# A four-layer kernel on one core: attention 0's keys are made ahead and its loop is unrolled; attention 1 sends its queries three units ahead instead of two

## The chip, the core and the metric

The kernel runs as one program on one core of a Trainium2 chip. Its engines run beside each other and meet only at semaphores: TensorE (PE, with its weight loads as PEld), VectorE (DVE), ScalarE (ACT), GpSimd (POOL) and SyncE (SP), which here only issues transfers. The metric is the time of one execution in microseconds (us). A difference of about 0.2% is what a measurement of this kernel can tell from none.

## The reference, cut to what matters

The input x is 4 batches of 512 tokens by 512 columns, the context 4 by 512 by 128. Four residual layers follow each other:

```python
x = x + tanh(g_xattn[0]) * attention_0(layernorm(x), ctx)
x = x + tanh(g_ffn[0])   * mixture_0(layernorm(x))      # 8 experts, 2 per token
x = x + tanh(g_xattn[1]) * attention_1(layernorm(x), ctx, ctx)   # 16 heads of 32
x = x + tanh(g_ffn[1])   * mixture_1(layernorm(x))      # 16 experts, 6 per token

def attention_0(p, k_v):            # per batch
    kv  = k_v @ W_k.T + b_k                             # 512 x 128
    sim = (p @ kv) @ kv.T * 512**-0.5                   # 512 x 512
    return softmax(layernorm_over_columns(sim) * gamma + beta)

def attention_1(q, k, v):           # 4 groups of 4 heads share keys and values
    probs = softmax(q_h @ k_g.T / sqrt(32))
    return concat(probs @ v_g) @ Wc.T + bc
```

## The kernel before, in words

**Order of work.** Each layer is a block with one program for each engine, written out by hand; an engine works through its own list and waits for semaphores by count. A block begins when all engines have left the one before. PSUM is one tile `ps` of eight banks.

**Attention 0** goes batch by batch (b = 0 to 3). VectorE first makes the layer norm's statistics of all four batches (`row_stats`: four BATCH_NORM_STATS, some operations on 128x4, and a square root that ScalarE makes in `deviation`). For a batch, `keys` makes kv: PE multiplies (L415), ScalarE adds the bias (L348), takes the mean (L351) and centres the keys (kc, L357), PE turns kv (L418) and ScalarE copies it (L353). ScalarE normalises the rows of x (xn, L130), PE turns them (L425) and ScalarE copies them to pT (L363). The product with kv (L429) is copied to oT (L367), and PE multiplies it with kc to scores in banks 0 to 3 (L436). ScalarE squares them (L373) and takes the deviation (L376); VectorE scales and shifts (L455, L461) and makes the negative maxima (nmx, L465); ScalarE takes the exponential (L381); VectorE adds the result to x (L476). PE's body is a hardware loop over b with keys, turn, product and scores in this order. In ScalarE's loop body the keys and pT of batch b+1 come between deviation and exponential of batch b. The keys and turned rows share banks 4 to 7. GpSimd meanwhile splits the first seven of the experts' weight chunks into high and low parts (L168 to L182) and SyncE stores them. Nothing in this attention prepares the layer norm of mixture 0: that block's own start makes the statistics of its batches (`NORMED` is 0 for mixture 0 and 3 for mixture 1).

**Mixture 0** begins with columns(0) (rows normalised by ScalarE, turned by PE, split into xhi and xlo), the router's logits(0) (L1526), the copy of these (lgT, L1347), columns(1) (L1537) and then the shared expert's products (L1558 up, L1576 down). After these come blocks of gathered tokens (L1634, L1650, L1669) with weights fetched expert by expert.

**Attention 1** has 16 units: unit u is batch u // 4 and group u % 4. A unit takes eight steps j. In a step ScalarE takes two exponentials (L792, L796), GpSimd subtracts for the low half (L738), and PE makes the next scores (L843), two raw products for maxima (L828, read by VectorE's reductions L972), and products with the values (L857). Three parts run ahead of their unit:

- the queries: GpSimd normalises the group's columns (xc, L686 and L694, step 5), PE turns them (L817, step 0), ScalarE makes qhi (L756, step 1), VectorE qlo (L961, step 2), and SyncE copies both into `qs` by three transfers (`strips`, L622 and L625). Unit u does this for u+2, and GpSimd's part for u+3.
- the raw products of unit u+2 begin at step 4 of unit u, and wait there for these transfers;
- the maxima of unit u+1 are turned at step 4 (L833), split, and sent by two transfers (L632) that the first scores of unit u+1 wait for.

Buffers of xc, qhi and qlo are two deep by group parity. `qs` has room for all 16 heads, so a unit's strips lie in the place of the unit four before it. During units 0 to 3 and 12 to 15 a second stream splits and stores the last 16 weight chunks.

Of the kernel before, what the change touches and what calls it, by code (L numbers as in the profile page):

```python
# [15 lines left out]
P = 128  # L16
B, S, D = 4, 512, 512
NT = B * S // P
TB = S // P
# [201 lines left out]
def cross_attention_0(nc, a, sb, g):  # L221
# [3 lines left out]
    with ExitStack() as ctx:  # L225
# [13 lines left out]
        kv = sb(ctx, "a0_kv", [P, TB, DC])  # L239
# [3 lines left out]
        kc = sb(ctx, "a0_kc", [P, S])  # L243
# [12 lines left out]
        def sem(name):  # L256
# [3 lines left out]
        gates_ready, gamma_done, nmean_ready, kc_ready = (  # L260
            sem(n) for n in ("gates", "gamma_done", "nmean", "kc"))
# [10 lines left out]
        with nc.Block() as block:  # L272
# [64 lines left out]

            def normalise_scalar(act, b):
                act.wait_ge(g["s_ln"], b + 1)
                for t in range(TB):  # L340

                    act.wait_ge(xn_read, TB * b + t + 1)
                    g["normalise"](act, xn, t, TB * b + t, 0, xn_ready)

            def keys_scalar(act, b):

                act.wait_ge(kvT_mm, b + 1)
                act.activation(kvT[:], ps[:, 4, :], ACT.Identity, bias=bk[:, 0:1],  # L348
                               accum_out=ksum[:]).then_inc(kvT_ready, 1)
                act.wait_ge(kvT_ready, b + 1)  # L350
                act.mul(nmean[:], ksum[:], -1.0 / S).then_inc(nmean_ready, 1)  # L351
                act.wait_ge(kv_tr, b + 1)
                act.copy(kv[:].rearrange("p t d -> p (t d)"), ps[:, 5, :]).then_inc(kv_ready, 1)  # L353

                act.wait_ge(nmean_ready, b + 1)
                act.wait_ge(sim_ready, TB * b + TB)
                act.activation(kc[:], kvT[:], ACT.Identity, bias=nmean[:, 0:1]).then_inc(kc_ready, 1)  # L357

            def turn_scalar(act, b):

                act.wait_ge(xn_read, TB * b + 2 * TB)
                for k in range(KD):
                    act.copy(pT[:, k, :], ps[:, 4 + k, :]).then_inc(pT_ready, 1)  # L363
# [5 lines left out]
            def deviation_scalar(act, b):  # L369
                for t in range(TB):  # L370

                    act.wait_ge(sim_ready, TB * b + TB + t + 1)
# [12 lines left out]
            def _(act):  # L385
                act.wait_ge(eps_set, 1)
                g["deviation"](act, 0, 0)
                act.wait_ge(par_in, PARAMS)
                normalise_scalar(act, 0)
# [8 lines left out]
                with act.Fori(0, B - 1) as b:  # L398
                    normalise_scalar(act, b + 1)
                    deviation_scalar(act, b)  # L400
                    keys_scalar(act, b + 1)
# [1786 lines left out]
```

## Time and profile before

| | |
|---|---|
| median of 3 runs | 2252.59 us (2250.19 to 2254.02) |
| profiled execution, its own time | 2243.46 us |
| its span | 2241.7 us |
| PE busy | 1911.8 us (85%) |
| POOL, DVE, ACT busy | 1004.7, 1167.9, 861.3 us |
| mean granted clock of TensorE | 0.925 of full speed |

The profiled execution is one run, and the others are timed without a profile. Busy shares are averages over four layers with different limits; the stages are: attention 0 to 123.4 us, mixture 0 to about 682, attention 1 to about 1172, mixture 1 to the end. An idle time in a row is the time the engine stood still before that instruction, with what ended it. "x4" marks merged instructions: the time is then that of the group.

### The profile page before, as it was taken

Reading aid. Unit: us, or ns where it says so; the run is one execution under the profiler, and the core shown is the slowest. Engines: PE = TensorE matmul, PEld = TensorE weight load, DVE = VectorE, ACT = ScalarE, POOL = GpSimd, SP = SyncE. Lnnn points to the kernel's source line nnn. Section 1 sums busy time; section 2 is a strip of 40 time slices with the busy share of each in tenths; the row PEclk is TensorE's granted clock in tenths of the full one; section 3 lists DMA queues with packets and bytes.
Section 4 is the critical chain, followed back from the end, with each engine's and each line's share of the span. In section 5 each row is a group of like instructions: output and inputs, shape, how many; then the busy total and the mean of one; then the engine's idle time right before and its main releaser. Section 6 shows DMA issues by size and latency. Waiting matters only on the chain. (4 is left out here: it accounts for less than half of the span.)

```text
span 2241.7 us, 36800 instructions
## 1 busy us (share of the span) xinstructions
PE 1911.8 (85%) x10825; PEld 1567.9 (70%) x10825; DVE 1167.9 (52%) x2331; ACT 861.3 (38%) x1403; POOL 1004.7 (45%) x735
## 2 busy tenths in 40 slices
PE   3758999979892777888868899999999979999995
PEld 2347787757671455555546777799999879899994
DVE  5474654423334896878973766444444334344442
ACT  3752221123341676767655123133333223233331
POOL 4344655625454787889631001143433323333331
PEclk9779999988895798998989999999999989999998
DMA  9367666988887574323642000766469895754444
GB/s 337 122 218 242 184 205 226 294 295 240 257 197 169 151 227 98 47 42 51 190 150 83 29 31 1 264 178 158 88 176 334 265 304 128 187 130 83 78 79 111
DMA packets 131457, 372.67 MB, mean 166 GB/s; under 512 B 20456, under 2 KB 24424, under 8 KB 126104
## 3 DMA queue, kind: packets, MB, share of 16 engines
q1 hardware_dynamic: 80504, 260.69, 36.3%
q0 software_dynamic: 33600, 79.73, 18.6%
q10 hardware_dynamic: 17184, 30.09, 3.8%
q8 instruction: 96, 1.57, 0.3%
q14 instruction: 73, 0.60, 0.1%
HBM read 209.93 MB, written 151.86 MB: 161 GB/s over the span
## 5 line engine op out<-in xcount | busy, mean ns | idle before, releaser
L1650 PE MATMUL ps<-f_wb,f_xThi 128*128 x2088 | 537.7, 339 | 29.9 <-issue 26.8
L1774 POOL DMA_INDIRECT y_scratch<-f_yo,f_rows x150 | 238.7, 1591 | 479.0 <-issue 264.1
L1650 PEld LDWEIGHTS ps<-f_wb,f_xThi 128*128 128x128 f32 x2088 | 372.0, 193 | 41.3 <-issue 32.3
L1650 PE MATMUL ps<-f_wb,f_xTlo 128*128 x1044 | 346.7, 332 | 0.0
L738 POOL TENSOR_TENSOR a_elo<-a_e,a_ehi 128x1024 f16<-128x1024 f32 x128 | 282.8, 2222 | 87.0 <-ACT a_ehi L796 85.0
L1669 PE MATMUL ps<-f_wb,f_hThi 128*128 (+2 forms) x822 | 276.9, 418 | 7.3 <-DVE f_hTlo L2049 7.3
L2067 DVE TENSOR_TENSOR f_g<-ps,f_bb 128x352 f32<-128x352 f32 x111 | 58.3, 525 | 337.2 <-PE ps L1650 334.4
L1747 POOL DMA_INDIRECT f_xg<-xn_scratch,f_rows x150 | 160.0, 1067 | 158.7 <-PE ps L1634 119.3
L1650 PEld LDWEIGHTS ps<-f_wb,f_xTlo 128*128 128x128 f32 x1044 | 200.9, 192 | 0.0
L1485 ACT ACTIVATE f_yo<-ps,f_share 128x512 f32<-128x512 f32 x150 | 103.2, 688 | 249.2 <-PE ps L1669 191.3
L972 DVE TENSOR_REDUCE a_nmax<-ps 128x1 f32<-128x512 f32 x256 | 163.9, 680 | 56.4 <-PE ps L828 56.0
L1558 PE MATMUL ps<-f_xhi,f_w13hi 128*128 128x512 f32 x448 | 175.7, 392 | 0.0
L1558 PE MATMUL ps<-f_xlo,f_w13hi 128*128 128x512 f32 x448 | 174.8, 390 | 0.0
L1558 PE MATMUL ps<-f_xhi,f_w13lo 128*128 128x512 f32 x448 | 174.7, 390 | 0.0
L1669 PEld LDWEIGHTS ps<-f_wb,f_hThi 128*128 128x128 f32 (+2 forms) x822 | 142.4, 191 | 42.3 <-issue 24.0
L1576 PE MATMUL ps<-f_w2hi,f_act_parts 128*128 128x512 f32 x448 | 153.0, 409 | 21.2 <-DVE x_res L2015 20.5
L828 PE MATMUL ps<-a_ks,a_qs 96*128 96x512 f32 x256 | 114.4, 515 | 61.1 <-DMA a_qs<-a_qlo 41.9
L792 ACT ACTIVATE a_e<-ps 128x1024 f32<-128x1024 f32 x128 | 132.7, 1036 | 82.5 <-PE ps L843 81.0
L1473 ACT CAST f_xThi<-ps 128x512 fp32r<-128x512 f32 x150 | 88.1, 587 | 195.1 <-PE ps L1634 187.7
L1669 PE MATMUL ps<-f_wb,f_hTlo 128*128 (+2 forms) x411 | 162.2, 395 | 0.0
L1479 ACT CAST f_hThi<-ps 128x384 fp32r<-128x384 f32 (+1 forms) x150 | 67.4, 449 | 207.5 <-PE ps L1659 202.7
L2049 DVE TENSOR_TENSOR f_hTlo<-ps,f_hThi 128x384 fp32r<-128x384 f32 (+1 forms) x150 | 78.4, 523 | 113.7 <-ACT f_hThi L1479 111.6
(242 smaller groups left out, 3654.1 us busy)
## 6 DMA issues: line engine op xcount, KB each, us to landing
f_wb<-w_scratch SPq DMA_DIRECT2D x16, 2816.0 KB
w_scratch<-f_stage_up SPq DMA_DIRECT2D x27, 1024.0 KB
w_scratch<-a_stage_up SPq DMA_DIRECT2D x23, 1024.0 KB, 5.3
f_stage_raw<-in_f_w_dram SPq DMA_DIRECT2D x29, 768.0 KB, 7.2
f_wb<-w_scratch SPq DMA_DIRECT2D x16, 1024.0 KB
w_scratch<-f_stage_down SPq DMA_DIRECT2D x108, 128.0 KB
f_wb<-w_scratch SPq DMA_DIRECT2D x8, 1536.0 KB
a_later_raw<-in_f_w_dram SPq DMA_DIRECT2D x16, 768.0 KB, 5.2
```

The source lines that it names most:

```text
L738: pool.tensor_tensor(l, e, h, ALU.subtract).then_inc(lo_pool, 1)
L792: act.activation(e32[:, j % 4, :, :], ps[:, 2 * (j % 2):2 * (j % 2) + 2, :], ACT.Exp)
L828: pe.matmul(ps[:, A_BANK + n % 2, :], qs[0:3 * HD, HPG * grp + q, P * t:P * t + P], ks[0:3 * HD, grp, :], start=True, stop=True).then_inc( ...
L972: dve.tensor_reduce(nmax[:, grp % 2, n:n + 1], ps[:, A_BANK + n % 2, :], AX.X, ALU.max, negate=True).then_inc(max_done, 1)
L1473: act.copy(xThi[:, b % 2, :, :].rearrange("p k t -> p (k t)"), ps[:, XB, :]).then_inc(xT_hi, 1)
L1485: act.activation(yo[:, b % 3, :], ps[:, OB + b % 2, :], ACT.Identity, scale=share[:, b:b + 1]).then_inc(yo_ready, 1)
L1558: mm = pe.matmul(ps[:, 2 * h + w, :], wt[:, h, w, k, :], xt[:, k, S * t:S * t + S], start=(m == 0), stop=(m == 3 * KD - 1))
L1576: mm = pe.matmul(ps[:, bank(c), :], at[:, t % 2, h, P * c:P * c + P], wt[:, h, :], start=(m == 0), stop=(m == 5))
L1650: mm = pe.matmul(out, xt[:, b % 2, k, :], weights(at, w, k, low), start=(m == 0), stop=(m == 3 * KD - 1))
L1669: mm = pe.matmul(ps[:, OB + b % 2, :], ht[0:n, b % 2, P * j:P * j + P], wb[0:n, bass.ds(at + 512 * NB + 1024 * j + 512 * low, D)], start=( ...
L1747: pool.indirect_dma_start(xg[:, b % 3, :], None, xn_d, bass.IndirectOffsetOnAxis(ap=rows_of[:, b:b + 1], axis=0), bounds_check=ROWS + SPAR ...
L1774: pool.indirect_dma_start(y_d, bass.IndirectOffsetOnAxis(ap=rows_of[:, b:b + 1], axis=0), yo[:, b % 3, :], None, bounds_check=ROWS + SPARE ...
```

## The change

1. **Attention 0's keys.** kv and kc get one place for each batch. PE makes keys 0 and 1, turns batch 0, and makes keys 2 and 3, all ahead of the first product; the keys use banks 4 to 7 in pairs, and batch 0 is turned into banks 0 to 3.
2. **Attention 0's loops** are written out (no hardware loop) on PE, ScalarE and VectorE. Batch b+1 is turned right behind the scores of batch b. A product waits for one k of pT at a time. VectorE's second pass waits tile by tile.
3. **Statistics for mixture 0.** VectorE makes `row_stats(1, b-1)` at the head of batch b, ScalarE its root beside the deviation of batch b. `NORMED` is 3 for both mixtures, so mixture 0's block makes only those of batch 3.
4. **Attention 1's queries** run one unit further ahead: unit u turns, splits and sends u+3, and GpSimd normalises u+4. Ahead of unit 0 three units are prepared instead of two.

```diff
-        kv = sb(ctx, "a0_kv", [P, TB, DC])
+        kv = sb(ctx, "a0_kv", [P, B, TB, DC])
-        kc = sb(ctx, "a0_kc", [P, S])
+        kc = sb(ctx, "a0_kc", [P, B, S])
...
             def deviation_scalar(act, b):
...
+                if b > 0:
+                    g["deviation"](act, 1, b - 1)
                 act.wait_ge(squared, TB * b + TB)
...
                 keys_scalar(act, 0)
                 g["deviation"](act, 0, 1)
+                keys_scalar(act, 1)
+                turn_scalar(act, 0)
                 g["deviation"](act, 0, 2)
-                turn_scalar(act, 0)
+                keys_scalar(act, 2)
                 g["deviation"](act, 0, 3)
+                keys_scalar(act, 3)
...
+                def product(b):
+
+                    if b == 0:
+                        pe.wait_ge(kv_ready, B)
+                    for k in range(KD):
+                        pe.wait_ge(pT_ready, KD * b + k + 1)
+                        mm = pe.matmul(ps[:, 4, :], kv[:, b, k, :], pT[:, k, :], start=(k == 0), stop=(k == KD - 1))
+                    mm.then_inc(oT_mm, 1)
...
+                for b in range(B):
+                    product(b)
+                    scores(b)
+                    if b + 1 < B:
+                        turn(b + 1)
...
+                for b in range(B):
+                    if b > 0:
+                        g["row_stats"](dve, 1, b - 1)
                     dve.wait_ge(sdev_ready, b + 1)
...
                 strips(1, 1)
                 load(2, 2)
+                strips(2, 2)
...
-                        if j == 1 and has_prepare:
-                            prepare_scalar(act, u + 2, (grp + 2) % GROUPS)
+                        if j == 1 and not (isinstance(u, int) and u + 3 >= UNITS):
+                            prepare_scalar(act, u + 3, (grp + 3) % GROUPS)
...
                 pe.wait_ge(qlo_ready, 1)
                 prepare_tensor(pe, 1, 1)
+                pe.wait_ge(qlo_ready, 2)
+                prepare_tensor(pe, 2, 2)
...
                 prepare_vector(dve, 0, 0)
                 prepare_vector(dve, 1, 1)
+                prepare_vector(dve, 2, 2)
                 dve.wait_ge(g["x_back"][2], 16)
                 g["row_stats"](dve, 2, 2)
                 maxima_vector(dve, 0, 0, range(16))
...
-    NORMED = B - 1 if layer == 1 else 0
+    NORMED = B - 1
```

On ScalarE, one turn of attention 0's loop stood so before (keys of the next batch, then pT, then exponentials):

```order
L376 ACT_TABLE_LOAD
L376 ACTIVATE a_sdev<-a_ssum,eps 128x4
L348 ACTIVATE a_kvT,a_ksum<-ps,a_bk 128x512
L351 ACTIVATE a_nmean<-a_ksum 128x1
L353 COPY a_kv<-ps 128x512
L357 ACTIVATE a_kc<-a_kvT,a_nmean 128x512
...
L363 COPY a_pT<-ps 128x512 x4
...
L381 ACT_TABLE_LOAD
L381 ACTIVATE a_y,a_den<-a_y,a_nmx 128x512
```

The same place for batch 1 now (L371 is pT, L386 the deviation, L391 the exponential):

```order
L125 ACT_TABLE_LOAD
L125 ACTIVATE std<-vraw,eps 128x4
L386 ACTIVATE a_sdev<-a_ssum,eps 128x4
L371 COPY a_pT<-ps 128x512 x4
L391 ACT_TABLE_LOAD
L391 ACTIVATE a_y,a_den<-a_y,a_nmx 128x512 x4
```

The four operations of the keys left the turn, and the root for mixture 0 (L125) came in under the same table load. Ahead of the first product ScalarE now has, between the root of batch 1 and the gates:

```order
L125 ACTIVATE std<-vraw,eps 128x4
L357 ACTIVATE a_kvT,a_ksum<-ps,a_bk 128x512
L360 ACTIVATE a_nmean<-a_ksum 128x1
L362 ACTIVATE a_kc<-a_kvT,a_nmean 128x512
L364 COPY a_kv<-ps 128x512
L371 COPY a_pT<-ps 128x512 x4
L125 ACTIVATE std<-vraw,eps 128x4
L357 ACTIVATE a_kvT,a_ksum<-ps,a_bk 128x512
L360 ACTIVATE a_nmean<-a_ksum 128x1
L362 ACTIVATE a_kc<-a_kvT,a_nmean 128x512
L364 COPY a_kv<-ps 128x512
L125 ACTIVATE std<-vraw,eps 128x4
```

Keys 1 stand ahead of pT, keys 2 behind the root of batch 2, and keys 3 follow the last root. At the start of attention 1 VectorE had two qlo ahead of the statistics and the sixteen reductions of unit 0:

```order
L961 SCALAR_TENSOR_TENSOR a_qlo<-ps,a_qhi 128x512 x2
L104 BN_STATS stats<-x_res 128x6 x4
...
L972 TENSOR_REDUCE a_nmax<-ps 128x1 x16
```

and has three now (L1001 and L1012 are these lines after the change):

```order
L1001 SCALAR_TENSOR_TENSOR a_qlo<-ps,a_qhi 128x512 x3
L104 BN_STATS stats<-x_res 128x6 x4
...
L1012 TENSOR_REDUCE a_nmax<-ps 128x1 x16
```

The third qlo moved in front of the statistics of batch 2.

## Rows read from the trace of the kernel before

**Rows 1.** Windows by stage: busy us of engines (instructions), clock, DMA share, GB/s.

```profile
123.40:437.00 313.60, 288.69 (x1301) 233.84 (x1302) 166.56 (x298) 85.85 (x144) 178.97 (x173) 0.95 0.72 236
437.00:682.00 245.00, 205.65 (x981) 163.46 (x979) 77.81 (x222) 82.78 (x176) 110.04 (x86) 0.90 0.86 240
```

**Rows 2.** Timeline (start, us, engine, line, idle before), before batch 0's product.

```profile
21.66 11.82 DVE L110 TENSOR_TENSOR mdif<-mdif 128x4 f32<-128x4 f32 x1
...
32.21 1.25 POOL L182 TENSOR_TENSOR a_stage_down<-a_stage_raw,a_stage_down 128x512 fp32r<-128x512 f32 x1
...
36.00 5.74 PE L429 MATMUL ps<-a_pT,a_kv 128*128 128x512 f32 x8 [14.97 <-ACT a_pT L363]
...
37.77 0.30 ACT L125 ACTIVATE std<-vraw,eps 128x4 f32<-128x4 f32 x1 [1.83 <-DVE vraw L112]
```

**Rows 3.** Timeline, one turn of attention 0's loop, 85.19 to 105.98.

```profile
85.19 0.60 ACT L367 ACTIVATE a_oT<-ps 128x512 f32<-128x512 f32 x1 [2.53 <-PE ps L429]
...
85.84 3.70 PE L436 MATMUL ps<-a_kc,a_oT 128*128 128x512 f32 x8 [0.69 <-ACT a_oT L367]
...
92.61 0.67 ACT L348 ACTIVATE a_kvT<-ps,a_bk 128x512 f32<-128x512 f32 x1
...
94.83 3.57 PE L425 MATMUL ps<-ident,a_xn 128*128 128x128 f32 x16 [0.75 <-ACT a_kv L353]
...
98.44 2.05 ACT L363 COPY a_pT<-ps 128x512 f32<-128x512 f32 x4 [3.11 <-PE ps L425]
...
98.90 0.27 DVE L465 TENSOR_SCALAR a_nmx<-a_mx 128x1 f32<-128x1 f32 x2
...
100.55 5.40 PE L429 MATMUL ps<-a_pT,a_kv 128*128 128x512 f32 x8 [2.14 <-ACT a_pT L363]
...
103.93 0.71 ACT L381 ACTIVATE a_y<-a_y,a_nmx 128x512 f32<-128x512 f32 x1
...
105.98 0.60 ACT L367 ACTIVATE a_oT<-ps 128x512 f32<-128x512 f32 x1 [1.25 <-PE ps L429]
```

**Rows 4.** Timeline, start of mixture 0.

```profile
123.39 1.28 ACT L125 ACT_TABLE_LOAD   x1 [2.83 <-PEq L272]
...
127.55 1.52 ACT L130 ACTIVATE f_xn<-x_res,nbias,rstd 128x512 f32<-128x512 f32 x2 [0.57 <-DVE nbias L118]
...
135.96 0.79 PE L1526 MATMUL ps<-f_xhi,f_gwhi 128*128 128x512 f32 x1 [3.87 <-DVE f_gwlo L2023]
...
143.64 0.56 ACT L1347 COPY f_lgT<-ps 128x512 f32<-128x512 f32 x1
...
144.26 3.67 PE L1537 MATMUL ps<-ident,f_xn 128*128 128x128 f32 x16 [3.82 <-ACT f_lgT L1347]
```

**Rows 5.** Timeline, start of attention 1.

```profile
692.45 2.47 DVE L104 BATCH_NORM_STATS2 stats<-x_res 128x6 f32<-128x512 f32 x4
...
696.32 0.16 DVE L118 SCALAR_TENSOR_TENSOR nbias<-msum,inv 128x4 f32<-128x4 f32 x1
...
715.90 1.22 PE L828 MATMUL ps<-a_ks,a_qs 96*128 96x512 f32 x2 [7.64 <-DMA a_qs<-a_qlo]
716.81 1.29 DVE L972 TENSOR_REDUCE a_nmax<-ps 128x1 f32<-128x512 f32 x2 [1.25 <-PE ps L828]
```

**Rows 6.** Waits in 737 to 1142: us in total, times, longest.

```profile
POOL a_elo L738 <- ACT a_ehi L796: 85.0, 57, 16.2
...
PE ps L828 <- DMA a_qs<-a_qlo: 34.2, 9, 8.3
```

**Rows 7.** Timeline, unit 4 of attention 1.

```profile
858.53 1.21 PE L828 MATMUL ps<-a_ks,a_qs 96*128 96x512 f32 x2 [8.30 <-DMA a_qs<-a_qlo]
...
864.20 2.13 POOL L738 TENSOR_TENSOR a_elo<-a_e,a_ehi 128x1024 f16<-128x1024 f32 x1 [4.63 <-ACT a_ehi L796]
```

**Rows 8.** Windows, one unit of attention 1 (unit 7).

```profile
917.30:939.50 22.20, 18.08 (x174) 13.20 (x172) 18.06 (x31) 15.66 (x21) 20.89 (x12) 0.92 0.34 47
```

**Rows 9.** Source line L738: ns min/median/max, first and last start.

```profile
L738 POOL TENSOR_TENSOR a_elo<-a_e,a_ehi x128: 2117/2138/2955, 737.1 to 1141.7; 128x1024 f16<-128x1024 f32 x128
```

More of the change, by code:

```diff
@@ L336, in _, with wait, turned_bank @@
                     stage.low(pool, i)
+            def wait(eng, s, value):
+                if value > 0:
+                    eng.wait_ge(s, value)
+            def turned_bank(b):
+                return 4 if b > 0 else 0
             def normalise_scalar(act, b):
@@ L433, in _ @@
                     for t in range(TB):
-                        pe.wait_ge(sim_used, TB * b + t + 1)
-                        pe.matmul(ps[:, t, :], oT[:, P * t:P * t + P], kc[:], start=True,
+                        wait(pe, sim_used, TB * (b - 1) + t + 1)
+                        pe.matmul(ps[:, t, :], oT[:, P * t:P * t + P], kc[:, b, :], start=True,
                                   stop=True).then_inc(sim_ready, 1)
+                pe.wait_ge(par_in, PARAMS)
+                keys(0)
+                keys(1)
+                turn(0)
+                keys(2)
+                keys(3)
+                for b in range(B):
+                    product(b)
+                    scores(b)
+                    if b + 1 < B:
+                        turn(b + 1)
             @block.vector
             def _(dve):
-                dve.sem_inc(sim_used, TB)
                 for b in range(B):
@@ L446, in _ @@
                 dve.wait_ge(gates_ready, 1)
-                with dve.Fori(0, B) as b:
+                for b in range(B):
+                    if b > 0:
+                        g["row_stats"](dve, 1, b - 1)
                     dve.wait_ge(sdev_ready, b + 1)
@@ L660, in unit @@
                         put(u - 1, 1)
-                    if has_prepare:
-                        strips(u + 2, (grp + 2) % GROUPS)
-                        if not (static and u + 3 == UNITS):
-                            load(u + 3, (grp + 3) % GROUPS)
+                    if not (static and u + 3 >= UNITS):
+                        strips(u + 3, (grp + 3) % GROUPS)
+                        load(u + 3, (grp + 3) % GROUPS)
                     if static and grp > 0:
@@ L712, in _ @@
                 pool.wait_ge(g["s_ln"], 2 * B + 1)
-                for u in range(2):
+                for u in range(3):
                     prepare_pool(pool, u, u, 0)
-                pool.wait_ge(xc_ready, 2)
+                pool.wait_ge(xc_ready, 3)
                 pool.memset(flt(ks[3 * HD:3 * HD + 2, :, :]), 1.0).then_inc(zero_set, 1)
@@ L730, in unit @@
                 def unit(u, grp, has_prepare, has_maxima, wc_batch):
-                    has_columns = has_prepare and not (isinstance(u, int) and u + 3 == UNITS)
+                    has_columns = not (isinstance(u, int) and u + 4 >= UNITS)
                     for j in range(8):
@@ L904, in unit @@
                     b = 0 if wc_batch is None else wc_batch + 1
+                    turns = not (isinstance(u, int) and u + 3 >= UNITS)
                     for j in range(8):
@@ L917, in unit @@
                             scores_tensor(pe, u + 1, (grp + 1) % GROUPS, 0)
-                        if j == 0 and has_prepare:
+                        if j == 0 and turns:
                             if last_job(grp, b):
```

81 lines of the change are left out of this document (39 added, 42 removed).

## The prediction

> **What bounds the kernel now.** I read the windows by stage first, then the timeline of the stages that the change touches, then the waits of attention 1. In mixture 0, from 123.4 to 437 us, PE is busy 288.7 of 313.6 us at a clock of 0.95, and in its second half the DMA engines are at 0.86 [rows 1]. These stages hardly have edits of their own, so they matter only as the place where time won ahead of them is kept or lost. Attention 0 is a chain through ScalarE, PE and VectorE in which none is full: one turn of its loop goes from one oT to the next, 85.19 to 105.98, 20.8 us [rows 3]. In attention 1 PE waits 34.2 us in nine pieces for the strips of queries, the wait that the change aims at, while GpSimd waits 85.0 us for ScalarE [rows 6]. But a unit such as the seventh lasts 22.2 us with GpSimd busy 20.9 of them, though PE stands still for strips in it too [rows 8]. So there GpSimd is the bound and PE's wait is mostly hidden.
>
> **Attention 0, ahead of the first product.** Before, the product of batch 0 began at 36.00, behind pT. The reason for that late start is one VectorE operation on 128x4 that took 11.82 us, from 21.66 to 33.48; it was let go when GpSimd's uninterrupted run of splits ended, at 32.21 + 1.25 = 33.46 [rows 2]. Now the product waits for all four kv. The last of them stands behind the root of batch 3, which was done at 37.77 + 0.30 = 38.07 [rows 2]. A set of keys takes 94.83 - 92.61 = 2.2 us from kvT to the point where PE goes on behind kv [rows 3]. So the product starts at about 40.3 us instead of 36.0: **+4.3 us**, if the stall of 11.82 us comes again. It has the same neighbours (same transfers in, same splits on GpSimd, the same statistics), and I take it that it does.
>
> A rule speaks against that. A VectorE operation with two SBUF inputs held up by GpSimd is in the trace, but for ten GpSimd instructions on end, 11.82 us. The Trainium skill, "SBUF — State Buffer", "Who interferes with whom", says that whoever comes first gets the shared ports for the whole instruction and the other blocks, which would let VectorE in at the end of one GpSimd instruction. By that rule no such stall should come again; what the time would be then is worked out as the first rival.
>
> **Attention 0, the three turns.** Set oT of batch b at 0 and read the turn of rows 3 from 85.19. The squares and the root end where kvT began, +7.4 (92.61). Then came keys, PE's turning and pT: pT's copies began at +13.25 (98.44), 3.11 us of it waiting for PE, and ended at +15.3; the product began at +15.4 and took 5.4 [rows 3]. Now PE turns the next batch behind the scores: scores end at +4.35 (85.84 + 3.70), turning takes 3.57, ready at +7.9. The copies follow at +8.0 to +10.05, the product starts behind the first of four, +8.6, and ends at +14.0. That is no longer the last thing: the exponentials need nmx, whose last came at 98.90 + 0.27, that is +14.0 [rows 3]. VectorE's chain starts from the root as before, about 0.4 later in batches 1 to 3, since it finishes the statistics first, less some 0.2 for the wait by tile. Two exponentials of 0.71 behind the last nmx [rows 3] give oT at +15.4 for the first turn and +15.8 for the others. ScalarE has no room to do it sooner, and **the exponentials behind VectorE are what is late next**. The statistics' first part (2.5 us and small operations, 4.0 us in all with its root [rows 5]) begins about 1.3 us into the turn, when x of the batch before is written, and is done by +5, ahead of the root at +7.4, so it is hidden; its cover is 1 to 2 us thin.
>
> Three turns: 15.4 + 15.8 + 15.8 = 47.0, plus 3 us of waits of VectorE for GpSimd, whose splits still fall into the first turns (an estimate: a small part of the 11.82 above). So 50. Before they took from the end of the first product (36.00 + 5.74 = 41.74) to 105.98, 64.2 us. **-14.2 us**; bounds: 17.2 with no waits, about 2.4 if one whole stall of 11.82 falls into the turns on top. The last batch has no successor and stays, give or take 0.5. Written-out loops in place of hardware loops I put at zero: of the branch and register work nothing shows on the chain between the rows.
>
> **Mixture 0's start.** The block began at 123.4 with a table load; the first xn came at 127.55, behind statistics of batch 0 [rows 4]. Those are there now, so xn starts some 0.2 behind the block's start: 4.0 earlier. PE's logits go with it: 135.96 to about 132. PE then had to wait 3.82 us for lgT, until 144.26; ScalarE made that copy at 143.64 only because it stood behind the root of batch 2, which VectorE delivered late [rows 4]. That root is gone too. PE finished the logits at 144.26 - 3.82 = 140.44, a copy and hand-over take about 0.8, so 3.0 more. **-7.0 us** for columns(1) and the shared expert behind it, whose weights are asked for at the block's start and must be cast and split by then: before, the cast came behind ScalarE's other work, so I have no row on how early it could. If that is late it takes the 3.0 back; the 4.0 falls too if the weights are the bound (lower bound 0). I take 7.0, the value the rows give.
>
> **Attention 1's start.** The third qhi goes into the buffer of the first, so ScalarE waits for the strips of unit 0 to land; PE's first raw product shows when, 715.90 [rows 5]. So qhi(2) and qlo(2) are made at 716.0 to 717.3, and VectorE, which before made the statistics of batch 2 while these strips flew, now makes them behind: 696.48 - 692.45 = 4.0 us for one such set, root included [rows 5]. The reductions of unit 0 begin at about 721.5 instead of 716.81, and everything of unit 0 hangs on them: **+4.7 us**. Queued behind this wait are on ScalarE the root of batch 2 and v_mid, on SyncE the strips of unit 2 and the parameters; their users come later than 721. Bounds: 0.5 (only qlo) and 8 (with GpSimd in the way, as at 21.66).
>
> **Attention 1's units.** With strips asked for one unit earlier all nine waits go, 34.2 us at most. What it is worth is read off GpSimd. In unit 4 PE waits 8.30 us, until 858.53, and GpSimd runs dry 4.63 us for it [rows 7], with a follower at the next unit's start: 6 us. In units like the seventh GpSimd idles 22.2 - 20.9 = 1.3 us in all [rows 8], not all of it for strips: four such units, 2 us together. Units 0 to 3 have splits on ScalarE and VectorE beside the chain, which hold it too; 3 us for the four, an estimate between 0 and the waits. The other units showed no such wait. **-11 us**; bounds 0 and 34.2.
>
> **Sum:** +4.3 - 14.2 - 7.0 + 4.7 - 11.0 = -23.2 us. Against the profiled execution's own 2243.5 that is 2220. The profiled execution was 9.1 us under the median of the runs, and I put the difference on the median, since the timed runs are what is compared: 2252.6 - 23.2 = 2229.4, say **2230 us**.
>
> **Rivals.**
> - *The long stall does not come again.* Then statistics and keys flow, and by the durations above the fourth kv is ready near 34: the product at 34 instead of 40.3, -6.4 more, 2223 us. For it: nothing else in the trace holds a VectorE operation for more than a GpSimd instruction or two. Against it: timings there hardly move.
> - *Strips were the bound.* All 34.2 us of attention 1 come back instead of 11: 2206 us. For it: 85.0 us of GpSimd's idle time [rows 6]. Against it: unit 7.
> - *The gain is eaten in mixture 0*, whose second half runs with DMA at 0.86 [rows 1]: if the experts' weights come when they come, the -16.9 of attention 0 and mixture's start vanish, and 2246 is left; with attention 1's start at its upper bound, no change. Against it: these transfers start relative to the stage as well.
> - *Slower: GpSimd's subtraction.* PE, with nothing to wait for, packs work closer to GpSimd's, and VectorE's two-input operations take the ports from it. L738 has a median of 2.138 us, and a worst case of 2.955 [rows 9]. If all 128 took 2.955, that is 128 x 0.817 = 105 us: 2334. It decides against the change from 2.138 + 23.2/128 = 2.32 us on.
>
> **How the numbers follow.** Forecast 0.52, no stall 0.20, strips 0.08, eaten 0.12, slower 0.08. The range leaves out the tails of the second and last: 2208 to 2246. About 0.2% (4.5 us) can be told from no change. Faster: forecast, the first two rivals and half of the third, 0.86; same: the other half, 0.07; slower 0.07.
>
> **What would show it.** In the new profile: a VectorE operation of over 5 us near 21 us, or none; first product near 40; three oT about 16 us apart; mixture 0's first xn directly at its start, and its second set of turned columns 14 us behind the block's start instead of 21 (144.26 - 123.39); reductions of attention 1 at 5 to 6 us behind the first raw product; no PE wait on a_qs<-a_qlo in the units; GpSimd's idle time in attention 1 down by about 11 us from 85, and its subtraction still at 2.14. I am wrong if the turns stay near 20 us, if the product's start moves by more than the keys, or if attention 1's units keep their pace while the strips' waits are gone.

## The result, and the profile of the changed kernel

The changed kernel takes 2244.07 us (median of 22 runs, 2230.30 to 2252.13), the kernel before 2252.83 us (22 runs, 2237.62 to 2262.72). The ratio is 0.9964, with a 95% interval of 0.9947 to 0.998: 8 us less (0.0036 x 2252.83), where 23.2 were forecast. The direction was right and the time lies inside the range, but nearly two thirds of the gain didn't come.

The profiled execution of the changed kernel took 2247.85 us (span 2246.0, clock 0.92), 4.4 us more than that of the kernel before. The last stage makes this difference, and its code is the same in both. From mixture 1's first block to the end it took 809.0 us before and 819.0 after, and 809 to 823 over all 17 kernels of this study, none of which edits it; the timed runs show no loss of this size, so I take it for scatter. So stages are compared here, not totals. Up to mixture 1's first block the changed kernel is 5.6 us ahead (1427.0 against 1432.65).

Attention 0, after (timeline: start, us, engine, line, operation; in brackets the idle time before and what ended it), answering to [rows 2, 3]:

```profile
26.52 7.50 DVE L117 TENSOR_SCALAR rstd<-inv 128x4 f32<-128x4 f32 x1
...
32.74 1.25 POOL L182 TENSOR_TENSOR a_stage_down<-a_stage_raw,a_stage_down 128x512 fp32r<-128x512 f32 x1
...
37.36 0.30 ACT L125 ACTIVATE std<-vraw,eps 128x4 f32<-128x4 f32 x1 [8.96 <-DVE vraw L112]
...
40.17 5.96 PE L450 MATMUL ps<-a_pT,a_kv 128*128 128x512 f32 x8 [0.68 <-ACT a_kv L364]
...
46.17 0.60 ACT L375 ACTIVATE a_oT<-ps 128x512 f32<-128x512 f32 x1 [4.54 <-PE ps L450]
...
61.27 0.57 ACT L375 ACTIVATE a_oT<-ps 128x512 f32<-128x512 f32 x1
...
81.14 0.57 ACT L375 ACTIVATE a_oT<-ps 128x512 f32<-128x512 f32 x1
...
97.12 0.57 ACT L375 ACTIVATE a_oT<-ps 128x512 f32<-128x512 f32 x1
```

The long VectorE operation has moved to another instruction and is there again, let go when GpSimd's run of splits ended (32.74 + 1.25 = 33.99). The first product starts at 40.17 (forecast 40.3). The four oT are 15.1, 19.9 and 16.0 us apart. From the end of the first product (40.17 + 5.96) to the fourth oT it takes 51.0 us, where 50 were forecast and 64.2 were needed before. No copy of oT after the first waits for PE any more; ScalarE comes to it behind the exponentials, as forecast.

The start of mixture 0, after, answering to [rows 4]; the block begins at 116.64:

```profile
124.89 1.05 ACT L1379 CAST f_w13hi<-f_wraw 128x1024 fp32r<-128x1024 f32 x1 [1.04 <-DMA f_wraw<-in_f_w_dram]
...
127.38 1.05 ACT L1379 CAST f_w13hi<-f_wraw 128x1024 fp32r<-128x1024 f32 x1 [1.45 <-DMA f_wraw<-in_f_w_dram]
...
132.41 0.81 ACT L130 ACTIVATE f_xn<-x_res,nbias,rstd 128x512 f32<-128x512 f32 x1 [1.66 <-DMA xn_scratch<-f_xn]
...
134.26 1.12 PE L1578 MATMUL ps<-ident,f_xn 128*128 128x128 f32 x4 [3.87 <-ACT f_lgT L1388]
```

PE still waits for the copy of the logits (lgT), 3.87 us where it was 3.82. ScalarE makes that copy behind casts and normalised rows that wait for transfers.

The seam in mixture 0 where its blocks begin, first after, then before:

```profile
433.37 0.61 POOL L172 CAST f_stage_down<-f_stage_raw 128x512 fp32r<-128x512 f32 x1 [2.55 <-DMA w_scratch<-f_stage_down]
...
436.44 1.29 POOL L182 TENSOR_TENSOR f_stage_down<-f_stage_raw,f_stage_down 128x512 fp32r<-128x512 f32 x1
...
438.05 1.28 POOL L1788 DMA_INDIRECT f_xg<-xn_scratch,f_rows  x1 [0.18 <-issue]
...
443.23 1.09 PE L1675 MATMUL ps<-ident,f_xg 128*128 128x128 f32 x4 [5.47 <-DMA f_xg<-xn_scratch,f_rows]
```

```profile
445.60 1.28 POOL L1747 DMA_INDIRECT f_xg<-xn_scratch,f_rows  x1 [0.18 <-issue]
...
449.70 0.52 PE L1634 MATMUL ps<-ident,f_xg 128*128 128x128 f32 x3 [1.66 <-DMA f_xg<-xn_scratch,f_rows]
```

Counted from mixture 0's start, PE comes to the first block 3.5 us earlier (321.1 against 324.6) and then waits 5.47 us instead of 1.66 for gathered rows. GpSimd asks for them behind its last split, and in both kernels its splits wait there for the stores of earlier ones (6.63 and 2.55 us in the last two chunks after, 6.55 and 2.59 before).

Attention 1's waits of PE, after, from 735 to 1137 (us in total, times, longest), beside [rows 6], and of before the rows that answer to them:

```profile
PE ps L894 <- DVE a_osum L1028: 25.6, 13, 3.4
PE ps L865 <- DVE a_nmax L1012: 24.5, 26, 2.0
PE ps L880 <- DMA a_qs<-a_mlo: 2.3, 3, 1.9
```

```profile
PE ps L828 <- DMA a_qs<-a_qlo: 34.2, 9, 8.3
PE ps L828 <- DVE a_nmax L972: 14.7, 19, 2.0
PE ps L857 <- DVE a_osum L988: 9.7, 6, 2.9
```

The 34.2 us for strips are gone, and 25.7 us of waits for VectorE have come ((25.6 - 9.7) + (24.5 - 14.7)). In units 0 to 3, VectorE's third subtraction of a chunk (line 182) tells why (ns min/median/max), before and after, 735 to 842:

```profile
L182 DVE TENSOR_TENSOR a_stage_down<-a_later_raw,a_stage_down x8: 678/1248/1819, 755.4 to 839.6; 128x512 fp32r<-128x512 f32 x8
```

```profile
L182 DVE TENSOR_TENSOR a_stage_down<-a_later_raw,a_stage_down x7: 679/2614/2623, 751.1 to 832.1; 128x512 fp32r<-128x512 f32 x7
```

```profile
783.88 2.18 POOL L775 TENSOR_TENSOR a_elo<-a_e,a_ehi 128x1024 f16<-128x1024 f32 x1
783.99 2.62 DVE L179 TENSOR_TENSOR a_stage_up<-a_later_raw,a_stage_up 128x512 fp32r<-128x512 f32 x1
...
787.82 5.10 POOL L775 TENSOR_TENSOR a_elo<-a_e,a_ehi 128x1024 f16<-128x1024 f32 x2 [1.76 <-ACT a_ehi L833]
...
788.33 2.61 DVE L182 TENSOR_TENSOR a_stage_down<-a_later_raw,a_stage_down 128x512 fp32r<-128x512 f32 x1
```

In the last fence, a timeline of after, VectorE's subtraction starts 0.11 us behind GpSimd's and ends 0.55 us behind it: 2.62 us for what takes 0.68 where it meets no GpSimd instruction. All 4 long ones of the kernel before and all 11 of the changed one start 0.04 to 0.51 us behind the start of a GpSimd subtraction and end 0.55 us behind its end.

### The profile page after: what moved, and what is told of

Its sections match the earlier page's. It is cut to its first block and busy times, and to the rows that moved or that the text cites. A ratio compares the mean times of both kernels' runs of the same rounds, so it can differ in the third digit from the quotient of the medians.

```text
span 2246.0 us, 36627 instructions
## 1 busy us (share of the span) xinstructions
PE 1924.3 (86%) x10825; PEld 1574.3 (70%) x10825; DVE 1166.9 (52%) x2331; ACT 860.3 (38%) x1402; POOL 1007.7 (45%) x735
## 5 line engine op out<-in xcount | busy, mean ns | idle before, releaser
L1691 PE MATMUL ps<-f_wb,f_xThi 128*128 x2088 | 541.1, 341 | 25.7 <-issue 20.3
L1691 PEld LDWEIGHTS ps<-f_wb,f_xThi 128*128 128x128 f32 x2088 | 374.9, 195 | 37.9 <-issue 28.9
L1012 DVE TENSOR_REDUCE a_nmax<-ps 128x1 f32<-128x512 f32 x256 | 163.6, 679 | 39.2 <-PE ps L865 39.0
L829 ACT ACTIVATE a_e<-ps 128x1024 f32<-128x1024 f32 x128 | 131.9, 1031 | 84.2 <-PE ps L880 84.0
L894 PE MATMUL ps<-a_v,a_ehi 128*128 128x97 bf16 (+1 forms) x1024 | 121.1, 223 | 37.3 <-DVE a_osum L1028 29.6
L894 PEld LDWEIGHTS ps<-a_v,a_ehi 128*128 128x128 f16 x1024 | 97.9, 106 | 76.9 <-DVE a_osum L1028 40.7
```

The source lines that it names most:

```text
L829: act.activation(e32[:, j % 4, :, :], ps[:, 2 * (j % 2):2 * (j % 2) + 2, :], ACT.Exp)
L894: mm = pe.matmul(ps[:, PV_BANK, P * t:P * t + VC], part[:, j % 4, i, P * t:P * t + P], v3[:, bass.ds(TB * b + 2 * (j % 2) + i, 1), grp, 0:VC],
L1012: dve.tensor_reduce(nmax[:, grp % 2, n:n + 1], ps[:, A_BANK + n % 2, :], AX.X, ALU.max, negate=True).then_inc(max_done, 1)
L1691: mm = pe.matmul(out, xt[:, b % 2, k, :], weights(at, w, k, low), start=(m == 0), stop=(m == 3 * KD - 1))
```

## The experiments

All times below are read at the same marks. *bl* is the first product of mixture 0's blocks, *m0* that block's start, *U* the first product of its shared expert. *mh* is when attention 1's first transposed maxima are sent, counted from its start. Units are counted from GpSimd's first subtraction of each. *u12-15* ends with the start of the last one. *long* counts VectorE's subtractions of chunks in units 0 to 3 (24, in all_three 21) that took over 1.9 us, and *sum* is the time of all; a record is missing in some. Each row of the table is one profiled execution.

```
kernel               m0     U-m0  bl-m0  bl    | mh   u0-3   u4-11  u12-15 | long sum
before               123.4  24.2  326.3  449.7 | 32.8 105.4  200.7   98.5  |  4   34.2
moved_before         123.0  24.2  321.2  444.3 | 32.5 106.6  200.5   98.4  |  3   32.2
low_first_before     122.9  24.2  326.0  448.9 | 32.4 108.0  200.4   94.5  |  8   34.7
blank_before         123.4  24.2  327.1  450.5 | 32.5 102.4  198.8   90.4  |
att0_only            117.7  21.1  328.5  446.2 | 31.5 105.2  201.0   98.4  |  4   33.0
att1_only            122.4  24.2  325.8  448.2 | 36.5 110.6  189.0   96.5  | 10   40.6
after                116.6  21.0  326.6  443.2 | 36.0 108.2  195.8   97.1  | 11   39.6
stats_back           113.3  23.8  329.6  442.9 | 36.0 113.4  191.9   96.9  | 13   44.5
hold_splits          108.1  20.5  325.8  434.0 | 35.9 113.5  192.0   96.8  | 14   44.5
moved_chunks         117.2  20.5  319.5  436.7 | 36.5 111.8  191.5   95.4  | 13   43.1
hold_and_moved       114.0  20.3  320.6  434.7 | 36.1 111.9  191.4   95.6  | 13   43.1
swap_start           120.0  20.7  326.8  446.8 | 34.0 112.0  191.6   97.1  | 13   43.0
all_three            118.1  20.9  320.5  438.6 | 34.0 105.3  188.7   97.4  | 11   38.0
low_first            116.4  20.7  328.3  444.6 | 36.0  97.6  186.8   88.4  |  5   29.9
moved_swap_low       119.6  20.6  319.3  438.9 | 34.0  96.3  196.8   88.3  |  7   33.5
hold_moved_swap_low  115.4  20.1  320.7  436.2 | 34.0 104.9  183.0   90.7  |  7   33.4
blank_after          115.0  20.2  329.1  444.1 | 36.1  91.4  187.0   88.0  |
```

**One part alone.** Attention 0's part with the statistics ahead of mixture 0 (att0_only), and attention 1's part (att1_only):

```diff
 # att0_only: the hunks below line 600 and the last one; attention 1 as before
-    NORMED = B - 1 if layer == 1 else 0
+    NORMED = B - 1
 # att1_only: the hunks of cross_attention_1
-                        strips(u + 2, (grp + 2) % GROUPS)
+                        strips(u + 3, (grp + 3) % GROUPS)
```

> The attention-0 part and the statistics ahead of mixture 0 alone; attention 1 as in the kernel before. Theory: this part ends attention 0 some 7 us earlier, mixture 0's shared stage starts 10 us earlier, but the blocks of mixture 0 start only 6 to 7 us earlier than before (443 instead of 449.7), since GpSimd's chain of splits ends at the same distance from the block's start. Time about 6 us under before, ratio 0.997. Rival (the forecast): 17 us of this part arrive, ratio 0.9925. Rival 2: nothing of it arrives, ratio 1.000.

> Attention 1's part alone, on the kernel before. Theory: it takes the strips' waits of PE away and gives about 3 us in the units, and loses as much at its start (first reductions later); attention 1 lasts 472 us in both, ratio 1.000. Rival (the forecast): start +4.7, units -11, attention 1 6 us shorter, ratio 0.997. Rival 2: it loses time, ratio over 1.001.

Measured: att0_only 2243.22 us, ratio 0.997 [0.9947, 0.9993]; att1_only 2246.32, ratio 0.9988 [0.9961, 1.0015], not told from no change. By the medians most of what arrived came from attention 0's part, though the two intervals overlap. Its 5.7 us at m0 were 3.5 at bl (446.2, where 443 was expected). Attention 1's part alone did as in the changed kernel: start later, units 0 to 3 longer, units 4 to 11 shorter. It lasted 467.0 us there against 472.2, nearer to the rival's 6 us less than to the theory's no change; over all seven kernels with three units ahead and the splits as they were it is 469.9, over the three with two 471.1.

**GpSimd held back** in attention 0 (hold_splits):

```diff
+                pool.wait_ge(g["s_ln"], B)
                 for i in range(AT_ONCE):
                     stage.high(pool, pool.tensor_copy, i)
```

> The changed kernel with GpSimd's splits of attention 0 held until the statistics of all four batches are done. Theory: the VectorE operation held for 7.5 us (26.5 to 34.0) was held by this run of splits, so it is gone, the first product starts near 34 instead of 40.2, and mixture 0 starts 4 to 6 us earlier than 116.6 (the splits then fall into the turns and cost some of it back). Rival: the long operation has another cause and comes again, product at 40. Rival 2: the product is early but the turns grow by as much, mixture 0 at 116 to 118.

Measured: 2237.8 us, ratio 0.994 [0.9914, 0.9966]. Its timeline:

```profile
29.82 0.17 DVE L117 TENSOR_SCALAR rstd<-inv 128x4 f32<-128x4 f32 x1
```

```profile
31.75 3.70 PE L451 MATMUL ps<-a_pT,a_kv 128*128 128x512 f32 x8 [0.80 <-ACT a_kv L365]
```

The same operation takes 0.17 us, the product starts at 31.75, 8.4 us earlier, and as much is left at m0 (108.1 against 116.6, where 4 to 6 were expected) and at bl (434.0 against 443.2). So the held operation is GpSimd's doing, and it was worth more than the rival in the prediction gave it (6.4). The product itself took 3.70 us instead of 5.96, why I can't tell; the turns behind it, into which the splits now fall, gave these 2.3 us back.

**Two chunks moved** from mixture 0 to attention 0, on the changed kernel (moved_chunks) and on the kernel before (moved_before):

```diff
-AT_ONCE = 7
+AT_ONCE = 9
-SHARED = 24
+SHARED = 22
```

> The changed kernel with two of the chunks of weights that GpSimd splits in mixture 0's shared stage (24) split in attention 0 instead (9 instead of 7). Theory: the end of GpSimd's chain of splits, not the shared stage, set the start of mixture 0's blocks; with two chunks fewer it ends before PE does, PE's wait of 5.47 us for the first gathered rows falls to 1 to 2, and the blocks start 323 us behind mixture 0's start instead of 326.6. Attention 0 may end 0 to 3 us later for its two more chunks. Time 1 to 4 us under the changed kernel. Rival: the blocks wait for the experts' weights or another transfer, and stay at 326 us behind the start.

> The kernel before with two chunks more in attention 0 (9) and two fewer in mixture 0 (22). Theory: here PE waited only 1.7 us for the first gathered rows, so the move is worth less than in the changed kernel (7 us): the blocks start 323 to 325 us behind the block's start instead of 326.3, and time is 1 to 4 us less. Rival: the two chunks' work costs the shared stage in itself, and their removal gives the same 7 us, blocks at 319 to 320 behind the start; then the seam did not eat the gain of the start, the shared stage has its pace from something else.

Measured: moved_chunks 2235.53 us, 0.9944 [0.9917, 0.9971]; moved_before 2246.95, 0.9974 [0.995, 0.9997]. The first block of moved_chunks:

```profile
436.70 0.52 PE L1675 MATMUL ps<-ident,f_xg 128*128 128x128 f32 x3 [1.05 <-DVE x_res L2056]
```

PE waits no longer for gathered rows, and bl - m0 falls by 7.1 us, twice what was expected: 4.4 are the wait (5.47 to 1.05), 2.7 are that PE comes sooner. In the kernel before it falls by 5.1, more than the theory said and less than the rival: 0.6 is the wait (1.66 to 1.05), 4.4 are what two chunks cost the shared stage itself. With two chunks fewer in both kernels, the changed one reaches the blocks 1.7 us sooner behind m0 (319.5 against 321.2), with all chunks it did not. So with all chunks the gain at U was lost in the wait behind GpSimd's queue, and without that wait half of the 3.7 us won at U (20.5 against 24.2) arrives; where the other half goes I can't tell.

**The statistics put back** into mixture 0 (stats_back):

```diff
-                if b > 0:
-                    g["deviation"](act, 1, b - 1)
-                    if b > 0:
-                        g["row_stats"](dve, 1, b - 1)
-    NORMED = B - 1
+    NORMED = B - 1 if layer == 1 else 0
```

> The changed kernel with the statistics for mixture 0 back where they were: none in attention 0, all four in mixture 0. Theory: mixture 0's shared stage starts 24 us behind its block's start instead of 21, and its blocks start at the same distance as in the changed kernel, 325 to 327 us, because GpSimd's splits set that; attention 0's turns are a little shorter (mixture 0 starts at 114 to 117). Time as the changed kernel within 2 us. Rival: the 3 us are on the path, the blocks start at 329 to 330 behind the block's start and the time is 3 us longer.

Measured: 2245.06 us, ratio 0.9955 [0.9937, 0.9973]; bl at 442.9 against 443.2. The time is the theory's, the way is half the rival's: bl - m0 is 3.0 us longer (329.6), but 329.1 and 328.5 were seen with the statistics ahead too, and attention 0 is 3.3 us shorter without them. In these single executions the statistics ahead of time cost in attention 0 what they give in mixture 0. In the prediction they were hidden there, but for 0.4 us in each turn that has them.

**The start of attention 1** in another order (swap_start); on ScalarE the root of batch 2 likewise:

```diff
-                prepare_vector(dve, 2, 2)
                 dve.wait_ge(g["x_back"][2], 16)
                 g["row_stats"](dve, 2, 2)
+                prepare_vector(dve, 2, 2)
```

> The changed kernel with the start of attention 1 in another order: the statistics of batch 2 (VectorE) and their root (ScalarE) ahead of the third unit's queries, as they fell in the kernel before. Theory: the first maxima were late because these statistics stood behind queries that wait for the strips of unit 0; the first transposed maxima, 36 us behind attention 1's start in the changed kernel and 31.5 to 32.8 before, come 3 to 4 us earlier, and attention 1 is shorter by as much, if its units keep their length. Rival: VectorE's two-input operation waits for GpSimd instead, and the start stays at 36. Total 2 to 4 us less, inside the error of the timing.

Measured: 2242.4 us, ratio 0.9929 [0.9891, 0.9967], from six runs; mh 34.0 instead of 36.0. Two of the 3.8 us come back, where 3 to 4 were expected (eight kernels with three units ahead and this start in its old order have 36.1 on average, five with two 32.3). The rest I take to be the third set of queries itself.

**VectorE's lower splits blanked** in attention 1, in both kernels:

```diff
-                        eng.tensor_tensor(self.part(i, w, 1), ...)
+                        eng.memset(flt(self.part(i, w, 1)), 0.0)
```

> The changed kernel; VectorE's lower halves of the weight chunks split in attention 1 (units 0 to 3 and 12 to 15) are set to zero by a memset instead of the subtraction of two SBUF inputs, so the lower halves of these 16 chunks are missing. Theory: units 0 to 3 got longer (from 105 to 108 to 113 us over the profiles taken) since these subtractions collide with GpSimd's, which now has less idle time; with them gone the four units fall to 101 or less, and to less than the same kernel with two units ahead. Rival: the length of units 0 to 3 comes from ScalarE's casts or the chunks' transfers, and stays over 106.

> The kernel before, with the same replacement (lower halves of the 16 chunks of attention 1 missing). Theory: here units 0 to 3 fall less, from 105.4 to about 103, since PE's wait for the strips gave GpSimd and VectorE room. Rival: they fall by the same amount as in the changed kernel, so the collisions are not what the change brought.

Measured: blank_after 2222.07 us, 0.9855 [0.9814, 0.9897]; blank_before 2232.09, 0.99 [0.9853, 0.9946]; two runs each. Units 0 to 3 take 91.4 us with three units ahead and 102.4 with two. With the subtractions they were 108 to 113.5 and 105.4. So without them the change is worth 11.0 us in these four units, and with them it costs about 6. Blanking takes away the subtractions' own time as well as the collisions, so by itself it shows only that VectorE's work is what stands in the way. With two units ahead VectorE's busy time in units 0 to 3 falls by 21 us (97.2 to 75.9) and the units by 3; with three it falls by 26 (99.3 to 73.7) and the units by 17.

**The lower splits ahead of the maxima** of the same step (low_first on the changed kernel, low_first_before on the other):

```diff
+                        stage.low(dve, *split_step(u, j, LOWER))
                         maxima_vector(dve, *ahead(u, grp, j, has_prepare, has_maxima))
                         if head:
                             head_vector(dve, *head)
-                        stage.low(dve, *split_step(u, j, LOWER))
```

> The changed kernel with VectorE's lower splits of attention 1 issued ahead of the maxima of the same step instead of behind them. Theory: in units 0 to 3 of the changed kernel these subtractions start together with GpSimd's (12 of 22 took 2.3 to 2.6 us instead of 1.25, 5 of 24 before) because both are released by the same step; issued elsewhere in the step they miss it more often: fewer than 8 long ones, and units 0 to 3 take 100 to 106 us instead of 108 to 113. Rival: they fall under GpSimd's subtraction wherever they stand, as GpSimd is busy most of the time, or the maxima are late by as much: 108 or more.

> The kernel before with VectorE's lower splits of attention 1 issued ahead of the maxima of the same step. Theory: only the change brought these subtractions under GpSimd's (4 of 24 long before, 10 to 15 after), so the order is worth little here: units 0 to 3 take 103 to 106 us (105.4 before), attention 1 465 to 472, and with this order in both kernels attention 1's part of the change is worth 22 us or more. Rival: the order in itself is worth it, units 0 to 3 fall to 98 and attention 1 to 450 or less here too; then the change is worth about the same few us in either order.

Measured: low_first 2222.58 us, ratio 0.987 [0.9825, 0.9915] (four runs); low_first_before 2250.78, ratio 0.9997 [0.9975, 1.0019]. Line 182 in units 0 to 3 and PE's waits of low_first (735 to 1137):

```profile
L182 DVE TENSOR_TENSOR a_stage_down<-a_later_raw,a_stage_down x8: 727/886/1524, 747.6 to 826.2; 128x512 fp32r<-128x512 f32 x8
```

```profile
PE ps L865 <- DVE a_nmax L1012: 23.8, 30, 1.8
PE ps L894 <- DVE a_osum L1028: 9.9, 4, 2.8
```

GpSimd's waits for ScalarE in attention 1, first after (735 to 1132), then low_first (733 to 1103):

```profile
POOL a_elo L775 <- ACT a_ehi L833: 80.6, 45, 15.0
```

```profile
POOL a_elo L775 <- ACT a_ehi L833: 49.4, 33, 15.0
```

The median falls from 2614 to 886 ns, the sum from 39.6 to 29.9 us, units 0 to 3 from 108.2 to 97.6 (100 to 106 expected). PE's wait for osum is back to where it was before the change, and GpSimd's idle time, which the change had left nearly as it was (84.2 to 80.6), falls to 49.4. On the kernel before the same order does nothing in all: units 0 to 3 took 108.0 us (103 to 106 expected), units 12 to 15 took 94.5 instead of 98.5. With it in both kernels, attention 1 lasts 443.0 us from its start to mixture 1's, against 470.3 (471.9 and 472.2 with the old order), and by the two ratios the change is worth (0.9997 - 0.987) x 2252 = 28.6 us, give or take 11 by their intervals. The two further kernels below that have this order and three units ahead took 449.8 and 447.7 us in attention 1, so 20 to 28 is the fair figure. And not all of it is the order: 9.0 of the 28.9 us between the changed kernel and low_first lie in units 4 to 11, which have no splits.

**Together.** hold_and_moved is hold_splits with moved_chunks. all_three adds swap_start and takes one chunk of unit 2 into attention 0 (AT_ONCE 10, LATER 15). moved_swap_low and hold_moved_swap_low add low_first and swap_start to moved_chunks and hold_and_moved.

> The changed kernel with both: GpSimd's splits in attention 0 held behind the statistics, and two chunks more in attention 0 (9), two fewer in mixture 0 (22). Theory: the two effects are at different places and add up: mixture 0 starts at 108 to 110, its blocks 319 to 321 us behind that, at 427 to 430 (changed kernel 443.2, before 449.7). Time 14 us under the changed kernel, ratio to before 0.989 to 0.991. Rival: nine held chunks reach the end of attention 0 or collide in its turns, and mixture 0 starts at 112 or later; ratio 0.992 to 0.994.

> As the run of both, and attention 1's start in the other order (statistics of batch 2 first), and one chunk fewer in attention 1 (15, unit 2 has one instead of two) and one more in attention 0 (10). Theory: attention 1's first maxima at 34 instead of 36 us, one chunk in units 0 to 3 is worth 20/8 = 2.5 us (111.8 to 91.4 with all eight subtractions gone), so 4 us less than the run of both, ratio 0.987 to 0.989. Rival: the tenth chunk reaches into the end of attention 0 and costs what the fifteenth saves; same time as the run of both.

> The changed kernel with three edits: two chunks more in attention 0 and two fewer in mixture 0, attention 1's start in the other order, lower splits ahead of the maxima. Theory: the three are at different places and add up: low_first's attention 1 of 443 less 2 is 441, and mixture 0's blocks start 7 us earlier than in it; ratio to before 0.983 (low_first 0.987). Rival: splits and GpSimd's subtraction fall together again after the start is shifted by 2 us, units 0 to 3 over 105, ratio 0.988 or more.

> As moved_swap_low, with GpSimd's splits in attention 0 also held behind the statistics. Theory: holding is worth 2 us here by the blocks' start (434.7 with both against 436.7), so the time is as moved_swap_low or 2 us less. Rival: held splits collide with the turns more than they free the first product, 2 us more.

Measured: 2234.79 us, 0.991 [0.9881, 0.9939]; 2227.48, 0.9881 [0.9846, 0.9917]; 2230.35, 0.9907 [0.9879, 0.9936]; 2219.16, 0.9851 [0.9819, 0.9883]. The effects don't quite add up. As the rivals of hold_and_moved and all_three had it, nine held chunks reach further into attention 0's turns (m0 114.0 against 108.1 with seven), ten more so (118.1). The one chunk less in unit 2 took units 0 to 3 from 111.9 to 105.3, more than its eighth. moved_swap_low's 0.9907 is not the 0.983 expected and no better than low_first's 0.987, though the two intervals overlap. In its profiled execution units 4 to 11, in which nothing differs, took 196.8 us instead of 186.8. In what rhythm VectorE and GpSimd meet changes from kernel to kernel, and I have no rule for it. hold_moved_swap_low beats both kernels, 1.5% under the one before; against low_first alone its lead isn't told by these intervals.

## Why the prediction was wrong

The sum was -23.2 us and the measured change -8. Two steps failed: mixture 0's start gave nothing instead of 7.0 us, and attention 1's units gave 4.8 instead of 11.0. Attention 0 was 3.1 short. Step by step, from the profiled executions and the table:

- *Attention 0, first product, +4.3:* right, 36.00 to 40.17. The stall came again as taken, on another instruction. (It was held before by twelve GpSimd instructions on end, from 22.76 to 33.46, not ten.)
- *Three turns, -14.2:* nearly right, 64.2 to 51.0 is -13.2. Without the statistics ahead the block is 3.3 us shorter (stats_back), so these were not hidden, as the step had said, but for 0.4 us a turn. The last batch, put at 0 give or take 0.5, lost 2.1: 97.12 to 116.64 is 19.5, 105.98 to 123.4 was 17.4. Attention 0 in all: -6.8 instead of -9.9.
- *Mixture 0's start, -7.0: the first step that failed.* The first xn started at once (116.70) as forecast, and logits 8.4 us behind the start, so the 4.0 came. The 3.0 did not: the step took the wait for lgT to be the root of batch 2 alone. That root was gone and PE waited 3.87 us, since ScalarE's casts waited 1.04 and 1.45 us for the shared expert's weights and the last xn ahead of lgT 1.66 for a transfer of an earlier one. The columns came 17.6 us behind the start instead of 14, U 3.2 us earlier instead of 7. None of these 3.2 reached the blocks: bl - m0 is 326.6 against 326.3, and in the four other kernels with this start and the same chunks, with nothing changed before it, 328.5, 326.8, 328.3 and 329.1. The prediction had no wait at that seam. This is the rival "eaten in mixture 0", at another place than it named: not the experts' weights, but GpSimd's splits ahead of the gathers. It took this term alone; attention 0's gain came through.
- *Attention 1's start, +4.7:* nearly right, 3.2 in the profiled pair and 3.8 over all kernels.
- *Attention 1's units, -11.0: the second step that failed.* "Splits on ScalarE and VectorE ... hold it too; 3 us for the four". Units 4 to 11 gave 8.8 us and units 12 to 15 gave 1.9 (means of seven kernels with three units ahead, 191.9 and 96.5, against 200.7 and 98.4 of three with two), 10.7 together. Units 0 to 3 lost 5.9 (111.6 against 105.7) where they should have won 3. The step took GpSimd for the bound and put VectorE at an estimate. In the changed kernel VectorE was the bound there, and before the change it was busy 98.48 of 107 us in them already:

```profile
735.00:842.00 107.00, 80.54 (x667) 57.15 (x668) 98.48 (x149) 80.56 (x106) 88.25 (x44) 0.85 0.71 196
```

This window of the kernel before (its third busy time is VectorE's) was the view to read, and I read the window of unit 7 instead [rows 8]. With the strips' wait gone, 10 to 14 of 24 subtractions were held by GpSimd's instead of 3 or 4. In all eleven kernels with the old order VectorE was idle for only 7.7 to 9.6 us of units 0 to 3, so what the holding added came out as length: a sum of 34.2 us and units of 105.4 before, 39.6 and 108.2 after, 44.5 and 113.5 in hold_splits, and 29.9 and 97.6 with the new order in low_first. My reading of why: PE's wait for strips kept the engines out of step, and without it ScalarE's exponentials released GpSimd's subtraction at the moment at which VectorE came to its own. That VectorE's subtractions ate the gain is shown by blanking them, and that it is their place in the step by moving them, each with its control on the kernel before. What sets the moment at which they meet is argued, not shown.

The granted clock of TensorE is a rival that the prediction didn't name. In units 0 to 3 it doesn't order the lengths: att0_only and swap_start both had 0.82 and took 105.2 and 112.0 us, low_first_before and low_first both had 0.87 and took 108.0 and 97.6. In units 4 to 11 of the kernels with three units ahead it does: 183.0 us at 0.99, 186.8 at 0.97, 191.5 at 0.96, 195.8 at 0.94, 196.8 at 0.93. Which of the two sets the other is not shown. With two units ahead they took 200.7 at 0.92 and 201.0 at 0.94, so at an equal clock the 8.8 us of these units are nearer 5.

The slower rival had the right pair of engines and the wrong victim: GpSimd's subtraction took 2.236 us on average (line 775 of the page; 2.222 before, the threshold was 2.32), it was VectorE that paid. The first rival, no long stall, was false for this kernel, and hold_splits shows that its price was set too low. "Strips were the bound" was false as it stood; yet with the lower splits issued first, attention 1's part of the change is worth 20 to 28 us, not far from that rival's 29.5 (34.2 - 4.7).

The parts as measured, -6.8 + 0.3 at the seam (both from the profiled pair) + 3.8 - 4.8 in the units (5.9 - 8.8 - 1.9, means over kernels), make -7.5 us, and the timed runs say 8. That the time came out inside the range is luck: its upper end, 2246, is a gain of no more than 6.6 us, and the two steps that make up the difference failed.

## What to carry to other kernels

When a change lets an engine run without a wait, look at every stage of the profile before for the engine that is nearly full there, and ask with which partner it will fall into step. Where VectorE has an operation with two inputs in SBUF beside a chain of GpSimd's, try it at another place of the step, and on both kernels: here a change that gave attention 1 about 1 us gave it 20 to 28 by it. And follow each gain to the next point at which an engine outside the chain must be done; here one was lost behind a queue of splits for which PE had hardly waited before.

## What the runs showed of the hardware

- A VectorE operation is held by GpSimd in two ways. In attention 1 it is held for one GpSimd instruction: 2.62 us beside one of 2.18, never more in units 0 to 3 than 2.65. That is how the Trainium skill, "SBUF — State Buffer", "Who interferes with whom", has it: the first gets the shared ports for its whole instruction. In attention 0, where GpSimd's instructions stand back to back, it was held through seven of them on end: 7.50 us for an operation of 0.17 (11.82 before, 9.47 in att0_only). Two forms were seen so, a multiplication of two tensors before and a TENSOR_SCALAR with a single tensor as input here and in att0_only. There the measurement disagrees with the rule as I read it, and with GpSimd held back the operation took 0.17.
- Another order of the same instructions went with 29 us of difference in attention 1 (471.9 to 443.0) in one kernel and 2 in the other (472.2 to 470.3). Of the 29, 9.0 lie in units 4 to 11, in which the order is the same.
- Units 4 to 11 of attention 1, without any edit in them, differ by up to 14 us among the kernels with three units ahead (183.0 and 196.8), the longer ones at the lower granted clock (0.99 and 0.93), so a gain that is read off one profiled execution there is good to some 7 us.
